# Differential attention gated by a routed two-expert layer on one core: regrouped normalisation, unread products and a halved last step

## What is computed

```python
xn = layernorm(x)                                   # every token
# attention, 8 heads of 16, over the 512 tokens of a block
p   = softmax(q @ k.T / 4)                          # q, k, v from xn
att = p @ v1 - lam * (p @ v2)                       # v1, v2: the two halves of the heads
s   = (0.2 * (layernorm(att) * ln_w + ln_b)) @ Wo + bo
# routed layer, over all 4096 tokens
h   = int(xn[:, 0] + xn[:, 1]) mod 8                # experts h and h+1, weight 1/2 each
f   = sum of (relu(xn @ W1[e] + b1[e]) @ W2[e] + b2[e]) / 2 over the two experts
out = x + s * silu(f)
```

## Time and profile before

| | |
|---|---|
| median of 3 runs | 409.66 us (409.14 to 410.87) |
| the profiled execution's own time | 411.52 us |
| its span from first to last instruction | 409.6 us |
| granted TensorE clock, mean | 0.991 |
| busy: PE, DVE, ACT, POOL | 381.5, 291.8, 267.5, 189.3 us |

### The profile page before, as it was taken

The page is one execution under the profiler, slowest core; times in us unless marked ns, Lnnn a source line. Parts: engine busy times, 40 slices in busy tenths (PEclk is TensorE's granted clock), DMA queues, the critical chain, the costliest instruction groups (busy, mean ns, idle before and its releaser), DMA issues.

```text
span 409.6 us, 8427 instructions
## 1 busy us (share of the span) xinstructions
PE 381.5 (93%) x2576; PEld 248.3 (61%) x2576; DVE 291.8 (71%) x758; ACT 267.5 (65%) x667; POOL 189.3 (46%) x262
## 2 busy tenths in 40 slices
PE   4996989999999999999999999999999999999993
PEld 2353876565775667766665668765676667764321
DVE  7787996656686757766676767866686767866884
ACT  3581756666765776576666767676766668675783
POOL 7944203454456543565355532663573444541200
PEclk9996999999999999999999999999999999999999
DMA  7975953263216451265105640346136141216740
GB/s 263 343 230 112 242 196 91 80 206 105 79 37 191 111 195 21 79 190 168 46 27 170 189 140 18 136 121 197 48 127 216 22 169 47 81 26 213 230 159 26
DMA packets 36945, 54.75 MB, mean 134 GB/s; under 512 B 6724, under 2 KB 25141, under 8 KB 36903
## 3 DMA queue, kind: packets, MB, share of 16 engines
q1 hardware_dynamic: 31456, 46.94, 34.6%
q0 software_dynamic: 3296, 6.76, 7.8%
q10 hardware_dynamic: 2151, 0.53, 0.6%
HBM read 15.59 MB, written 6.75 MB: 55 GB/s over the span
## 4 chain that ended last, share of the span: by engine, by line
PE 74%; DVE 7%; DMA 5%; ACT 4%; SPq 4%; issue 4%; POOL 1%; ACTq 0%; DVEq 0%; POOLq 0%
PE ring L1393 14%; PE pv_bank L1327 13%; PE ring L1414 12%; PE score L1289 12%; PE exp L1314 10%; PE ring L1251 3%; DVE neg_max L1049 3%; DMA xs<-xn_rows,inverse 3%; SPq L532 2%; PE ring L1335 2%; PE ring L1255 1%; PE ring L1353 1%; PE ring L1276 1%; PE ring L1375 1%; PE score L1264 1%
## 5 line engine op out<-in xcount | busy, mean ns | idle before, releaser
L1049 DVE TENSOR_REDUCE neg_max<-score 128x1 f32<-128x512 f32 x256 | 169.0, 683 | 72.3 <-PE score L1289 66.7
L1289 PE MATMUL score<-ks,qs 96*128 96x512 bf16 x256 | 98.3, 386 | 6.3 <-DVE neg_max L1049 6.0
L787 ACT ACTIVATE probs<-exp 128x512 f32<-128x512 f32 x124 | 72.5, 605 | 36.3 <-PE exp L1314 32.3
L787 ACT ACTIVATE xin<-exp 128x512 f32<-128x512 f32 x120 | 69.7, 604 | 38.5 <-PE exp L1314 38.1
L1314 PE MATMUL exp<-qs,ks 99*128 99x512 bf16 x244 | 91.7, 380 | 0.1
L825 ACT ACTIVATE hT<-ring,pair 128x128 f32<-128x128 f32 x256 | 73.4, 377 | 13.0 <-PE ring L1393 11.9
L1414 PEld LDWEIGHTS ring<-w_sb,hT 128*128 128x128 f32 x568 | 73.5, 191 | 10.4 <-issue 3.5
L1414 PE MATMUL ring<-w_sb,hT 128*128 (+1 forms) x568 | 75.4, 275 | 0.9 <-ACT hT L825 0.9
L1393 PEld LDWEIGHTS ring<-xsT,pair 128*128 128x128 f32 x512 | 66.3, 191 | 14.6 <-issue 8.1
L1393 PE MATMUL ring<-xsT,pair 128*128 128x128 f32 x512 | 68.2, 276 | 1.7 <-issue 1.2
L684 POOL TENSOR_SCALAR tanh<-tanh 128x128 f32<-128x128 f32 x32 | 17.2, 536 | 95.5 <-ACT tanh L845 95.2
(11 more groups left out here) (198 smaller groups left out, 417.4 us busy)
## 6 DMA issues: line engine op xcount, KB each, us to landing
pair<-table SPq DMA_DIRECT2D x32, 580.0 KB
qs<-parts SPq DMA_DIRECT2D x42, 128.0 KB
ks<-parts SPq DMA_DIRECT2D x42, 128.0 KB
xin<-_attn_hidden_states_dram SPq DMA_DIRECT2D x8, 256.0 KB, 4.4
table<-in_L_ffn_W_dram SPq DMA_DIRECT2D x2, 1024.0 KB, 9.2
w_sb<-in_L_ffn_W_dram SPq DMA_DIRECT2D x8, 256.0 KB, 10.4
xn_rows<-xn SPq DMA_DIRECT2D x8, 256.0 KB, 3.0
table<-_attn_hidden_states_dram SPq DMA_DIRECT2D x8, 256.0 KB, 5.4
```

Of the source, the lines that this page charges most:

```text
L787: a.activation(prob(n), exp_banks[n][:, :], ACT.Exp, scale=SCALE).then_inc(exp_done, 1)
L1049: v.tensor_reduce(neg_max[:, b % 2, col:col + 1], score_bank[n % 2][:, :], AX.X, ALU.max, negate=True).then_inc(max_taken, 1)
L1289: t.matmul(score_bank[n % 2][:, :], qs[0:MAX_ROW, b % STK, hh, c * P:(c + 1) * P], ks[0:MAX_ROW, b % STK, hh, :], start=True, stop=True).t ...
```

## The change

**Normalisation.** The last group (6, 8) is split into (6, 7) and (7, 8). POOL makes `shift` for the groups of blocks 0 to 3 as before, but for blocks 4 to 7 only once, after the last power. Block 4 is normalised on ACT. The order of ACT's normalisations is now 0, 1, 2, 4, 3.

**Routing.** DVE adds minus twice the mean before the power is ready, so `count_groups` needs no shift; conversions between integer and float are dropped where an operand may be of the other type; the running count is taken from a table that starts one column to the left, which leaves out one subtraction. `route` 1 on PE stands ahead of `peel` (0,1,2) and `transpose_x` 1. The second product of `find_tokens` goes to ACT.

**Peels, ones, unread products.** `peel` (1,0,2) moves behind score 1, `peel` (1,1,2) behind score 5; both stood ahead of `invert`. `ones` moves from ACT's queue to SP's. Five products of scores' shape, whose result nobody reads, are put on PE: one each behind scores 2, 3 and 4, and two behind `peel` (1,1,2).

**Extra tiles.** They start one score later (`FFN_FIRST`), their transposes 0.4 unit later. In the static part (t from 34 to 256) the order of PE, DVE, POOL and SP is unchanged; on ACT eleven of the `tanh` steps move behind the following exponential or copy.

**Closing.** Exps 252 to 255 are done in two halves of 256 columns, products and exponentials; the last group's value products are done in halves, each half in a bank of its own (`pv_bank` and score bank 1), so the exponent products from 240 on rotate over three banks and wait for the exponential n-3. `copy_o`, `turn_o`, the division, the statistics and `turn_z` of the last group are done per half.

The core of the diff:

```diff
-LN_GROUPS = ((0, 1), (1, 2), (2, 4), (4, 6), (6, 8))
-POOL_NORM = (4, 5, 6, 7)
+LN_GROUPS = ((0, 1), (1, 2), (2, 4), (4, 6), (6, 7), (7, 8))
+POOL_NORM = (5, 6, 7)
+LATE_SHIFT = 4
+EARLY_GROUPS = 3
...
-SHIFT_AT = (-58.5, -57.5, -55.5, -53.5, -50)
-NORM_AT = (-58, -56.4, -49.9, -47.93, -49.2, -49.1, -49, -48.95)
+SHIFT_AT = (-58.5, -57.5, -55.5, -53.5, -53.4, -50)
+NORM_AT = (-58, -56.4, -56.3, -48.61, -48.7, -48.68, -48.66, -48.63)
...
-QKV_AT = (-57.9, -50, 35, 67, 99, 131, 163, 181)
+QKV_AT = (-57.9, -48.62, 35, 67, 99, 131, 163, 181)
...
-PEEL_AT = (((-55.5, -55.3), (-55.4, -55.25)), ((-45.5, -45.3), (-45.4, -45.2)))
-STACK_AT = (((-55.58, -55.45, -55.28), (-55.57, -55.35, -55.2)), ((12.1, 12.3, 12.5), (12.2, 12.4, 12.6)))
+PEEL_AT = (((-55.5, -55.3), (-55.4, -48.65)), ((-45.5, 1.5), (-45.4, 5.3)))
+STACK_AT = (((-55.58, -55.45, -55.28), (-55.57, -55.35, -48.64)), ((12.1, 12.3, 12.5), (12.2, 12.4, 12.6)))
...
-TOKENS_AT = -45
+TOKENS_AT = -45.6
...
-EXTRAS_AT = 5.2
-GROUPS_AT = (9.05, 10.72, 13.05, 14.05)
+EXTRAS_AT = 5.9
+GROUPS_AT = (9.05, 10.72, 12.55, 14.05)
...
-FFN_FIRST = 7.6
+FFN_FIRST = 8.6
...
-TX, DX = 2.4, 3.2
+TX, DX = 3, 3.2
...
-INIT_AHEAD = 1.5
+INIT_AHEAD = 1.67
...
-SPLIT_MAX, TURN_MAX = 16.8, 18.9
+SPLIT_MAX, TURN_MAX = 16.5, 18.9
...
-TANH, GATE = 0.7, 1.84
+TANH, GATE = 1, 1.84
...
+WARM_AT = ((2.5, 1), (3.5, 1), (4.5, 1), (5.4, 2))
+LAST_GROUP = NT * HEADS - 16
+SPLIT_FROM = NT * HEADS - 4
+HALF_AT = (0.05, 1.05, 2.05, 2.9, 3.1, 3.2, 3.3, 3.4)
+LAST_PV = (0.1, 1)
+LAST_COPY = (0.8, 1.1)
+LAST_TURN = (2.5, 2.9)
+LAST_NORM = (2.55, 3.1)
+LAST_Z = (2.82, 3.4)
+LAST_STD = (2.85, 3.45)
+LAST_PROJECT = (3.3, 3.6)
+SQRT_AT = 2.75
...
-            at(n + LAG + EXP_OFF, "exp", n)
+            if n < SPLIT_FROM:
+                at(n + LAG + EXP_OFF, "exp", n)
+            else:
+                for half in range(HALVES):
+                    at(SPLIT_FROM + LAG + HALF_AT[4 * half + n - SPLIT_FROM], "exp_half", n, half)
+            if n >= SPLIT_FROM:
+                continue
...
+            if last:
+                continue
...
+    for half in range(HALVES):
+        t = NT * HEADS + LAG
+        at(t + LAST_PV[half], "pv_half", half)
+        at(t + LAST_COPY[half], "copy_half", half)
+        at(t + LAST_TURN[half], "turn_half", half)
+        at(t + LAST_NORM[half], "norm_last", half)
+        at(t + LAST_STD[half], "std_last", half)
+        at(t + LAST_Z[half], "turn_z", B - 1, half)
+        at(t + LAST_PROJECT[half], "project_o", B - 1, half)
+        at(t + LAST_PROJECT[half] + 0.01, "finish", B - 1, half)
...
+    for time, products in WARM_AT:
+        at(time, "keep_busy", products)
...
-        onehot = work[:, 512:768].rearrange("p (e t) -> p e t", e=EXP)
-        seen = work[:, 768:1024].rearrange("p (e t) -> p e t", e=EXP)
+        onehot = work[:, 511:767].rearrange("p (e t) -> p e t", e=EXP)
+        seen = work[:, 767:1023].rearrange("p (e t) -> p e t", e=EXP)
...
-        exp_banks = [exp_bank[n % 2] if n < DRAIN else last_banks[(n - DRAIN) % 4] for n in range(NT * HEADS)]
+        exp_banks = [exp_bank[n % 2] if n < DRAIN else last_banks[(n - DRAIN) % 4] if n < LAST_GROUP
+                     else last_banks[(n - LAST_GROUP) % 3] for n in range(NT * HEADS)]
         pv_bank = bank("pv_bank")
+        last_pv = [pv_bank, score_bank[1]]
...
+                elif kind == "ones":
+                    sp.wait_ge(dve_consts, 1)
+                    for slot_b in range(STK):
+                        sp.dma_start(ks[MAX_ROW:KROWS, slot_b, :, :],
+                                     ones_bf[:, :].unsqueeze(1).to_broadcast([PARTS, HEADS, S])).then_inc(ones_stacked, 16)
...
-                    if end < B:
+                    if first < LATE_SHIFT:
...
-                    if end < B:
+                    if first < LATE_SHIFT:
                         pool.wait_ge(rstd_ready, s[1] + 1)
                         g.tensor_tensor(shift[:, tok], shift[:, tok], rstd[:, tok], ALU.mult).then_inc(shift_ready, 1)
+                    if end == B:
+                        late = slice(C * LATE_SHIFT, NT)
+                        pool.wait_ge(rstd_ready, len(LN_GROUPS))
+                        link(g.tensor_scalar(shift[:, late], mv[:, late, 0], -1.0, None, ALU.mult))
+                        g.tensor_tensor(shift[:, late], shift[:, late], rstd[:, late], ALU.mult).then_inc(shift_ready, 1)
+                        pool.wait_ge(shift_ready, EARLY_GROUPS + 1)
...
+                elif kind == "tokens":
+                    act.wait_ge(in_tile_ready, 1)
+                    a.activation(token[:, 1, :, :, :], in_tile, ACT.Copy, scale=row_of[:, 0:1]).then_inc(token_ready, 1)
...
+                elif kind == "exp_half":
+                    n, half = s[1:]
+                    act.wait_ge(exp_filled, n + 1 + 4 * half)
+                    act.wait_ge(pv_done, n // 4 - PR // 4 + 1)
+                    a.activation(prob(n)[:, columns_of(half)], half_bank(n, half), ACT.Exp,
+                                 scale=SCALE).then_inc(exp_done, 1)
...
+                    act.wait_ge(pv_done, 4 * grp + 4 + half)
+                    act.wait_ge(shared_filled, fills[("turn_o", grp - 2)])
+                    a.activation(oT[:, grp % 2, columns_of(half)], last_pv[half][:, 0:S // 2],
+                                 ACT.Copy).then_inc(o_copied, 1)
...
+                dve.wait_ge(rstd_ready, len(LN_GROUPS))
                 link(v.tensor_tensor(v01[:, :], v01[:, :], rstd[:, :], ALU.mult))
-                dve.wait_ge(shift_ready, len(LN_GROUPS))
-                link(v.scalar_tensor_tensor(v01[:, :], shift[:, :], 2.0, v01[:, :], ALU.mult, ALU.add))
...
                 v.tensor_scalar(sign[:, :], v01[:, :], 0.0, 2.0, ALU.is_ge, ALU.mult)
-                link(v.tensor_copy(n_abs[:, :], whole_i))
-                link(v.tensor_tensor(over, n_abs[:, :], v_abs[:, :], ALU.is_gt))
-                link(v.tensor_tensor(n_abs[:, :], n_abs[:, :], over, ALU.subtract))
-                link(v.scalar_tensor_tensor(h[:, :], sign[:, :], -1.0, n_abs[:, :], ALU.add, ALU.mult))
-                link(v.tensor_copy(whole_i, h[:, :]))
-                link(v.tensor_scalar(whole_i, whole_i, EXP - 1, None, ALU.bitwise_and))
-                link(v.tensor_copy(h[:, :], whole_i))
-                link(v.tensor_tensor(onehot[:, :, :], h[:, :].unsqueeze(1).to_broadcast([P, EXP, NT]),
+                link(v.tensor_tensor(over, whole_i, v_abs[:, :], ALU.is_gt))
+                link(v.tensor_tensor(n_abs[:, :], whole_i, over, ALU.subtract))
+                link(v.scalar_tensor_tensor(h_i[:, :], sign[:, :], -1.0, n_abs[:, :], ALU.add, ALU.mult))
+                link(v.tensor_scalar(h_i[:, :], h_i[:, :], EXP - 1, None, ALU.bitwise_and))
+                link(v.tensor_tensor(onehot[:, :, :], h_i[:, :].unsqueeze(1).to_broadcast([P, EXP, NT]),
...
-                flat = work[:, 768:1024]
-                link(v.tensor_tensor_scan(flat, work[:, 512:768], zeros,
-                                          0.0, ALU.add, ALU.add))
-                v.tensor_tensor(seen[:, :, :], seen[:, :, :], onehot[:, :, :], ALU.subtract).then_inc(seen_ready, 1)
+                v.tensor_tensor_scan(work[:, 768:1024], work[:, 511:767], zeros,
+                                     0.0, ALU.add, ALU.add).then_inc(seen_ready, 1)
...
                 dve.wait_ge(slots_split, 1)
-                link(v.tensor_tensor(in_tile, by_pair(slot_tile[:, 0:NT], FT), over_pairs(columns[:, :, :], NT // 2), ALU.is_equal))
-                v.tensor_tensor(token[:, 0, :, :, :], in_tile, by_pair(ordinal[:, :], FT), ALU.mult)
-                v.tensor_scalar(token[:, 1, :, :, :], in_tile, row_of[:, 0:1], None, ALU.mult).then_inc(token_ready, 1)
+                v.tensor_tensor(in_tile, by_pair(slot_tile[:, 0:NT], FT), over_pairs(columns[:, :, :], NT // 2),
+                                ALU.is_equal).then_inc(in_tile_ready, 1)
+                dve.wait_ge(in_tile_ready, 1)
+                v.tensor_tensor(token[:, 0, :, :, :], in_tile, by_pair(ordinal[:, :], FT), ALU.mult).then_inc(token_ready, 1)
...
+                    link(v.tensor_tensor(v01[:, :], xin[:, :, 0], xin[:, :, 1], ALU.add))
                     dve.wait_ge(stats_ready, end)
-                    v.scalar_tensor_tensor(shift[:, tok], mv[:, tok, 0], -1.0, rstd[:, tok],
-                                           ALU.mult, ALU.mult).then_inc(shift_ready, 1)
+                    v.scalar_tensor_tensor(v01[:, :], mv[:, :, 0], -2.0, v01[:, :],
+                                           ALU.mult, ALU.add).then_inc(pair_summed, 1)
...
+                    o4 = shared[:, 0:n * P].rearrange("p (c i w) -> p c i w", c=n, w=VW)
+                    inv = inv_sum[:, first * HALF:(first + n) * HALF]
+                    link(v.reciprocal(inv, shared[:, 0:n * P].rearrange("p (n w) -> p n w", w=VW)[:, :, HD]))
...
+                elif kind == "keep_busy":
+                    for _ in range(s[1]):
```

(25 more changed lines are left out.)

94 lines of the change are left out of this document (59 added, 35 removed).

## The result

On one chip, in turns, the changed kernel took 408.94 us in the median of 20 runs and the kernel before 410.57: a ratio of 0.9967, with a 95% interval from 0.9952 to 0.9983. It is faster, but by the ratio only by 1.4 us where 3.1 were forecast (409.66 to 406.6), and so within the 0.5% that count as no change. Timed again twice, each time on a different chip, it gave 0.9981 [0.9941, 1.0021] and 0.9981 [0.9955, 1.0007]; both intervals reach beyond 1. The ratios leave out runs that took over 1.5% more than the fastest of the same kernel: one of these 20, and two of the 12 in the second repetition, where the profiled execution (415.5 us) is one of them, so that nothing is read from its trace. The opening does gain 2.0 us, of 3.4 forecast. Two places behind it then take back what the sum had as kept: the handover to the static part, and the closing.

The account below looks back on a forecast made before the run. PE was taken as the bound from 60 us on, PE and DVE together from 40 to 60. Span 409.6 - 3.4 (opening) + 0.3 (closing) = 406.5 us, so a median of 406.6 us; range 404.9 to 408.9.

Parts of the forecast that it names:

- Opening, DVE and PE: Opening: shorter DVE routing and two peels moved behind `invert` make `inverse` ready near 28.7 us instead of 31.15.
- Gather: Opening: the first tile's gather starts at 29.1 instead of 31.45 us, its first transpose at 34.1, 2.3 us earlier.
- I take the stores as just in time: Opening: the `xn_rows` stores, with DMA full until about 28.6 us, were assumed not to delay the first tile's gather.
- the gather still takes 4.89: Opening: the first tile's gather was assumed to keep its length of 4.89 us.
- Rival 2: Opening: late `xn_rows` stores or ACT token copy keep the gather in place, PE stays at 2.4 GHz; 408.2 us, chance 0.12.
- The clock: Opening: 2.4 GHz throughout, PE idle 0.3 us instead of 2.40; limited by DVE, the opening gains 3.4 us in all.
- rival 1: Opening: the clock falls all the same, so only the gather's 2.3 us counts, less the closing; 407.7 us, chance 0.14.
- The sign that was named for DVE as the bound: End of the opening: first store of `z` near 40.8 us would show DVE as the bound.
- SP's queue moves by the same 3.4, and so does the static part's first start value: Handover to the static part: the opening's 3.4 us gain passes whole through SP's queue to the first start value.
- Static part: From the handover to 378 us only eleven `tanh` steps differ: change 0, wrong if it moved over 1 us.
- Closing: Last exponentials, value products and following steps in halves: the end moves by +0.3 us, between -0.2 and +3.2.
- rival 4: Closing: halves cost what wholes do, about 4.0 us lost in place of 0.3; 410.3 us, chance 0.06.

Follow-up runs that it names:

- e5: Changed kernel with the first two `w2` loads issued behind the `xn_rows` stores and `ones` instead of ahead of all SP steps; 412.90 us, ratio 1.0019 to the kernel before.
- e11: New opening, old closing, no unread products, third weight pair four scores later, plus first two `w2` loads behind the stores; 411.64 us, ratio 0.9978 to the kernel before.
- e6: Changed kernel with the third pair of weight tiles loaded four scores later, behind the last stores of `z`; 410.03 us, ratio 0.996 to the kernel before.
- e9: Changed kernel run again, nothing edited, on a different chip; 410.62 us, ratio 0.9981 to the kernel before.
- e3: Kernel before with only the halved closing added; 410.76 us, ratio 1.0019 to the kernel before.
- e12: Kernel before with only the third pair of weight tiles loaded four scores later; 412.59 us, ratio 1.0015 to the kernel before.
- e1: Changed kernel without the five unread products; 408.72 us, ratio 0.9963 to the kernel before.
- e4: Changed kernel with six more unread products on PE ahead of the ninth `turn_tile`; 408.44 us, ratio 0.995 to the kernel before.

## Why the prediction was wrong

**Opening, DVE and PE: right.** `inverse` was forecast near 28.7, with 28.5 to 29.2 as the sign for it, and stood at 29.17; DVE's `count_groups` began 0.18 later than before where 0.04 was worked out. `route` and the peels went as written, and the peels moved behind `invert` fill PE from 32 to 34.

**Gather: the step that failed first.** Two terms were put at nothing: "I take the stores as just in time", and "the gather still takes 4.89". The last store was issued at 25.63 (25.8 forecast), but landed at 29.16, where it had landed before, so POOL's earlier end brought nothing, and the stores held the gather by 0.6 us. It started 1.4 us earlier instead of 2.3, and took 5.7 us to the first transpose in place of 4.9. `inverse`, 0.5 later than forecast, would have let it start near 29.5 and not at 29.1. Together that makes the first transpose 35.72, not 34.1; PE's idle time of 1.40 us in front of it stayed just under the 1.5 that the forecast had named as its refutation. Rival 2 had the stores' part of the mechanism, but with no move of the gather at all. Why the stores landed no earlier is open. The same bytes would end at the same time if DMA is the bound, and its share from 28 to 29 us fits that. But in all executions with `w2` in its old place the landing lies between 28.5 and 29.7, with the old opening as with the new; with these loads put off it was 28.07 in `e5` and 28.97 in `e11`. What made the gather itself longer isn't shown either.

**The clock: right in the opening, not for the rest.** It stayed full from 34 to 41 us with 1.40 us of idle time. What it was to bring beyond the gather's lead came as well: 1.1 us in the sum (3.4 - 2.3), 1.4 measured (a lead of 2.03 at score 28, with a first transpose only 0.67 earlier). So rival 1's mechanism was out. DVE remains nearly full from 40 to 60 us, 19.34 us of 20 where it had been 19.21, as the forecast had it. The 1.4 us that are missing at score 28 fit the 1.6 by which the first transpose is late. The sign that was named for DVE as the bound, the first store of `z` near 40.8, didn't come: it went out at 42.69, 1.5 us earlier than before and not 3.4. What the forecast didn't see is that PE runs dry at a second place.

**"SP's queue moves by the same 3.4, and so does the static part's first start value": failed.** SP's queue moved by 1.5 us, from the first store of `z` (44.16 to 42.69) to the last (61.53 to 60.06). The last two stood behind a weight load that costs the queue 2.3 us, and landed 2.8 to 3.2 us after issue, so the start value's gather moved by 1.2; POOL held the ninth tile's gather behind it. From score 28 to 32 0.8 us of lead were lost. The idle time that arose, 1.36 us, stood in front of the clock's fall, another 1.6, as in 3 of 8 executions. `e6` put the pair behind and kept 3.4 us: the figure of the forecast, by another way, and with an opening that was 0.9 us ahead of this one's without an edit that touches it.

**Static part, "0": a term without bounds.** It was -1.5 us in the profiled execution of after and +1.9 in `e9`, without an instruction moved. The forecast said that it would be wrong if this part moved by over 1 us; it does so from one execution to the next of the same kernel, so one profile of each can't price 1 us at the end.

**Closing: +0.3, measured +0.6.** The terms that the forecast writes out add up to +0.9 (0.3 + 0.4 - 0.5 - 0.2 + 0.9), so the 0.6 that the halves save by running one ahead of the other stood in its sum without a working. Two of its terms were off, in different directions. The start of a value step isn't paid twice: the two halves took 1.00 us, so the 0.4 fell away, and rival 4 with it. The Trainium skill ("TensorE: Matmul & The Clock Gate", Part 3) says that a weight load overlaps running products only where the row group differs. By that rule eight more weight loads per step would have been in the open; the 1.00 us speak against it here. What the closing lost instead is seen on PE and ACT of the kernel after in the last step, for the earlier trace rows:

```profile
397.94 0.64 PE L1406 MATMUL pv_bank<-xin,va 128*32 128x256 f32 x8
398.39 0.61 PE L1406 MATMUL score<-xin,va 128*32 128x256 f32 x8
...
399.26 0.38 ACT L845 ACTIVATE xin<-exp 128x256 f32<-128x256 f32 x1 [0.76 <-PE exp L1420]
...
399.81 0.67 ACT L845 ACTIVATE xin<-exp 128x256 f32<-128x256 f32 x2
...
401.63 1.28 ACT L864 ACT_TABLE_LOAD   x1
...
403.04 0.36 ACT L877 ACTIVATE zT<-ring 128x256 f32<-128x256 f32 x1
```

The next to last value step stands on PE in the middle of the half exponent products, so that ACT, with halves to do, runs dry for 0.76 us. The last exponential ends 11.36 us after the start of that of score 240, against 9.71 before (400.02 - 390.31, for the end): +1.65. The halved last steps give 1.05 of it back. And ACT's load of the table for the square root, 1.28 us, which before lay in a gap, is now in front of the first half's copy of `zT`, for which PE waits 0.58 us; the chain of waits runs through it. The forecast had counted neither.

**The sum, then.** Over the eight profiled executions with the new opening and the old pair the mean lead at score 36 is 1.1 us (-0.30 to 2.38), falls near 70 included; 0.6 goes in the closing. That leaves 0.5, where 1.4 us were measured in 20 runs and 0.8 in each of two repetitions. All leads refer to one profile of before, which seems a fast one: at score 36 the two other executions with its opening were level with it (`e3`) and 1.0 us behind (`e12`). That would close part of the gap; it isn't shown. The static part needn't come into it: where it was short (`e1` to `e4`), the kernel before took 410.1 us on the same chip, and where it was longer 411.8 to 412.0, so it went with the chip more than with the kernel. The clock has a part in what is left: over the 19 runs of the kernel after that count the mean granted clock lies between 0.987 and 0.999, and 0.01 less goes with 3.2 us more (correlation -0.79). One fall of 3.4 us to half is 0.004 of the span. (A slip in the forecast besides: by its own rule, half of rivals 1 and 2 each way, the chance of faster adds up to 0.76, not 0.73.)

## What to carry to other kernels

When work in front of a serial handover gets faster, write down what each queue behind it still has ahead of the handover: here one weight load on SP, 0.5 us to issue and 2.3 with what the queue does for it, and one gather on POOL took back much of a gain for which a dozen steps had been moved. Putting the load behind brought no time in the kernel before. In the new one the lead went down by 1.4 us between scores 28 and 36 in the mean of eight executions with the load in front, and by nothing in the mean of five with it behind. Don't count on a transfer to land sooner because it is issued sooner: here the last store landed at 29.16 all the same. And before halving the last step of a pipeline, lay the halves and the remaining whole steps in order on each in-order engine: the gain of the tail was less than the stall that the order made.

## What was not expected of the hardware

- The clock came down a second time, to 0.50 for 3.4 us, behind an idle time of TensorE of 1.36 us in an otherwise dense stretch, and in another kernel not behind 1.66 us; there with idle times up to 1.28 us it was never seen, in the opening not up to 1.40.
- A fall costs about 1.6 us where 3.4 us are at half clock.
- The same gather of 128 rows took 4.1 to 6.6 us from its start to the first transpose; why isn't shown.
- Sixteen matmuls of 256 columns with 32-column weights took the 1.00 us that eight of 512 columns take.
- With one order of instructions on TensorE, the 314 us of the static part differ by up to 4.2 us (312.0 to 316.2); the four shortest shared a chip.
